# GpSimd waits, at every fourth gather, for the group of four gathers before

## What is computed

```python
# layer 0, graph attention, 8 heads of 64; h = relu(layernorm(x))
feat = h @ W[head]
logit = leaky_relu(alpha_s[src] + alpha_d[dst], 0.2)
att = segment_softmax(logit, by=src)
x = x + relu(segment_sum(att[:, None] * feat[dst], by=src))
# layer 1; h = relu(layernorm(x)), xn = batchnorm(h)
agg = segment_sum(xn[src], by=dst) / max(degree, 1)
conv = relu(agg @ W_conv + b_conv)
attn = linear_attention(h, over 256 rows) @ Wo, taken back by position
x = x + batchnorm(conv + attn + h)
```

## Time and profile before

| | |
|---|---|
| median of 3 runs | 3542.48 us |
| lowest and highest | 3540.49, 3546.79 us |
| the profiled execution, its own time | 3542.78 us |
| its span | 3541.0 us |
| mean granted TensorE clock | 0.883 of full speed |
| busy: TensorE, VectorE, GpSimd, ScalarE | 2699.5, 2161.8, 1858.0, 995.2 us |
| gathers of the first stage (L506), first and last start | 880, 411.5 to 1865.1 us |
| gathers of the second stage (L1133), first and last start | 784, 2070.4 to 3237.6 us |

### The profile page before, as it was taken

The page is one execution under the profiler, slowest core; times in us unless marked ns, Lnnn a source line. Parts: engine busy times, 40 slices in busy tenths (PEclk is TensorE's granted clock), DMA queues, the critical chain, the costliest instruction groups (busy, mean ns, idle before and its releaser), DMA issues. The chain is left out here.

```text
span 3541.0 us, 46052 instructions
## 1 busy us (share of the span) xinstructions
PE 2699.5 (76%) x10647; PEld 1671.1 (47%) x10692; DVE 2161.8 (61%) x3783; ACT 995.2 (28%) x3078; POOL 1858.0 (52%) x1883
## 2 busy tenths in 40 slices
PE   6887377777777877777777787877778788788991
PEld 4554256666656656655656652323333333233440
DVE  9999966666666767666668743333333333334668
ACT  6733334444443444434444520000000000000220
POOL 0000255555555556555555446666666666664667
PEclk8998678898988899898898897888889999999995
DMA  5110366666666666666665856666666666565226
GB/s 184 47 40 31 111 180 185 186 189 185 180 182 188 180 191 189 183 192 176 177 189 191 288 152 174 176 180 178 178 176 178 173 173 175 171 174 157 67 66 251
DMA packets 243449, 588.25 MB, mean 166 GB/s; under 512 B 57744, under 2 KB 82832, under 8 KB 243400
## 3 DMA queue, kind: packets, MB, share of 16 engines
q0 software_dynamic: 133120, 443.52, 43.8%
q1 hardware_dynamic: 110280, 144.14, 12.4%
HBM read 533.43 MB, written 54.10 MB: 166 GB/s over the span
## 5 line engine op out<-in xcount | busy, mean ns | idle before, releaser
L506 POOL DMA_INDIRECT big<-feat_table,idx x880 | 841.3, 956 | 1020.8 <-ACT idx L531 407.5
L1133 POOL DMA_INDIRECT big<-h_table,idx x784 | 743.6, 948 | 460.6 <-issue 235.2
L801 PE MATMUL psA<-big,onehot 128*128 128x260 f32 x1760 | 504.0, 436 | 120.1 <-DVE big L683 95.4
L801 PE MATMUL psB<-big,onehot 128*128 128x260 f32 x1760 | 479.8, 420 | 18.6 <-DVE acc L693 13.1
L801 PEld LDWEIGHTS psA<-big,onehot 128*128 128x128 f32 x1760 | 365.4, 216 | 208.3 <-issue 115.2
L557 ACT ACTIVATE big<-big,late_weights 128x65 f32<-128x65 f32 x1760 | 434.4, 343 | 0.0
L801 PEld LDWEIGHTS psB<-big,onehot 128*128 128x128 f32 x1760 | 351.5, 209 | 84.9 <-DVE acc L693 22.2
L531 ACT CAST idx<-minorB 128x8 int32 (+1 forms) x101 | 20.4, 204 | 1142.6 <-DMA big<-h_table,idx 1142.6
L1565 DVE TENSOR_TENSOR acc<-acc,psCD 128x512 f32 x176 | 120.7, 686 | 320.1 <-remote 106.2
L1565 DVE TENSOR_TENSOR acc<-acc,psA 128x512 f32 x176 | 120.7, 686 | 273.6 <-remote 103.3
L1859 PE MATMUL psA<-big,onehot 128*128 x352 | 199.3, 650 | 58.9 <-issue 42.7
(11 more groups left out here) (447 smaller groups left out, 3960.8 us busy)
## 6 DMA issues: line engine op xcount, KB each, us to landing
nodes_all<-slot_nodes SPq DMA_DIRECT2D x56, 512.0 KB
big<-feat_table,idx POOLq DMA_INDIRECT x880
feat_table<-big SPq DMA_DIRECT2D x49, 264.0 KB, 2.1
x_table<-acc SPq DMA_DIRECT2D x49, 256.0 KB, 3.8
h_table<-big SPq DMA_DIRECT2D x49, 256.0 KB, 4.0
big<-h_table,idx POOLq DMA_INDIRECT x784
big<-h_table SPq DMA_DIRECT2D x49, 256.0 KB, 2.6
big<-x_table SPq DMA_DIRECT2D x49, 256.0 KB, 4.3
```

Of the source, the lines that this page charges most:

```text
L506: g.indirect_dma_start(ring[:, b.k, q * SB + u, :], None, feat_table, bass.IndirectOffsetOnAxis(ap=idx[:, 2 * b.k + q, u:u + 1], axis=0)). ...
L801: ins = pet.matmul(psum[:, 512 * hf:512 * hf + HALF_W], onehot[:, q, u % SB, :], ring[:, b.k, u, HALF_W * hf:HALF_W * (hf + 1)], start=(u ...
L1133: g.indirect_dma_start(big[:, place:place + D], None, h1_table, bass.IndirectOffsetOnAxis(ap=idx[:, r.c % CHUNK_CYCLE, b:b + 1], axis=0)). ...
```

## The change

GpSimd gets one more wait at each fourth gather of a group (gathers 3, 7, 11 and 15 of a batch, 3 and 7 of a row): for the landing of the four gathers of the group before. At that point the three gathers of its own group have been issued after those. Each wait is followed by an increment of `hold`. The first group of each stage has no wait.

```diff
         def layer0_gpsimd(pool):
+            def wait_group_before(b, group):
+                if group > 0:
+                    pool.wait_ge(rows_arrived[b.k * ARRIVAL_GROUPS + group - 1], b.pair(16 * ARRIVAL_GROUP, 16 * ARRIVAL_GROUP))
+                elif b.c > 0:
+                    last = Batch(b.i, b.c - 1)
+                    pool.wait_ge(rows_arrived[last.k * ARRIVAL_GROUPS + ARRIVAL_GROUPS - 1],
+                                 last.pair(16 * ARRIVAL_GROUP, 16 * ARRIVAL_GROUP))
+                elif b.i is not None:
+                    pool.wait_ge(rows_arrived[2 * ARRIVAL_GROUPS - 1], b.pair(16 * ARRIVAL_GROUP, 0))
+                else:
+                    return
+                pool.sem_inc(hold, 1)
...
+                            if (q * SB + u) % ARRIVAL_GROUP == ARRIVAL_GROUP - 1:
+                                wait_group_before(b, (q * SB + u) // ARRIVAL_GROUP)
                             g.indirect_dma_start(ring[:, b.k, q * SB + u, :], None, feat_table,
...
+            def wait_half_before(r, hf):
+                if hf == 1:
+                    group = 2 * r.c % GROUPS1
+                    pool.wait_ge(h_arrived[group], r.turn(64, 64 + arrived_before[group]))
+                elif r.c > 0:
+                    group = (2 * r.c - 1) % GROUPS1
+                    pool.wait_ge(h_arrived[group], Row(r.i, r.c - 1, CHUNK_CYCLE).turn(64, 64 + arrived_before[group]))
+                elif r.i is not None:
+                    pool.wait_ge(h_arrived[GROUPS1 - 1], r.turn(64, arrived_before[GROUPS1 - 1]))
+                else:
+                    return
+                pool.sem_inc(hold, 1)
...
                     for b in range(4 * hf, 4 * hf + 4):
+                        if b == 4 * hf + 3:
+                            wait_half_before(r, hf)
                         place = places[(r.c * SB + b) % RING1]
                         g.indirect_dma_start(big[:, place:place + D], None, h1_table,
```

## The result

The kernel before took 3541.12 us (median of 10 runs, 3529.73 to 3555.16) and the changed one 3556.65 us (10 runs, 3548.09 to 3570.18): a ratio of 1.0048, 95% interval 1.0029 to 1.0068. The change costs 0.5%. The forecast was 3545.0, a gain or loss that could not be told from none, with 3537 to 3554 as its range and 0.82 on "same"; the result is slower by more than its interval, and 2.65 us outside the range.

What follows compares the result with a forecast made beforehand. Second-stage gather issue on GpSimd was taken to be close to the path. Terms 0.6 + 0 + 4 + 0 = 4.6 us on GpSimd, counted at 55%, gave +2.5 us: 3545.0 us, range 3537 to 3554.

Steps and rivals of the forecast that it cites:

- Steps 1 and 2: Second stage: landing 3.70 us plus launch 0.8 us passes before the gather is due at 5.01; two late, 0.6 us.
- rival B: Waits end late: launch of 1.6 us would cost 134 free second-stage groups 0.3 us each, 40 us; chance 0.06.
- rival C: Fewer queued gathers land sooner, 3.43 instead of 3.70 us, 26 us faster in the second stage; chance 0.04.
- Step 3: Added instructions on GpSimd's sequencer: some 0.1 us per group, hidden by running gathers, 0 us; upper end 20 us.
- rival A: GpSimd's sequencer pays at the end of each loop turn in the second stage: 26 us slower; chance 0.08.
- Step 4: Second stage: eight sequencer pauses of 2.4 us show by 0.8 us each with less run-ahead; 4 us on GpSimd.
- Step 5: First stage: waits pass in time, even beside SP's node loads, and 5 us slack per batch absorbs delays; cost 0.
- The share of 55%: Part of GpSimd's 4.6 us delay taken to reach the kernel's time, since waits for freed places shorten: +2.5 us.
- The signs: Second stage: gathers 1.25 us apart, next to no DMA idle, landings 3.7 us, about 8 pauses, at most 1182 us.

Runs made afterwards that it cites:

- e17: The changed kernel again, on a chip where the kernel before takes 3006.45 us: 3080.02 us, ratio 1.0244.
- e3: Kernel before plus the change's waits in both stages, each for the group before the previous one: 3565.99 us, ratio 1.0032.
- e5: Kernel before plus eight increments of `hold` ahead of each fourth gather, both stages, no waits: 3574.65 us, ratio 1.0084.
- e10: Kernel before plus eight increments of `hold` ahead of each third gather, both stages, no waits: 3572.17 us, ratio 1.0083.
- e9: Kernel before plus one increment of `hold` ahead of each fourth gather, both stages, no waits: 3541.88 us, ratio 0.9997.
- e13: Kernel before (3003.62 us on this chip) plus waits for the group three before, ahead of each fourth gather: 3003.95 us, ratio 0.9999.
- e18: The code of e5 on a chip where the kernel before takes 3006.45 us: 3005.37 us, ratio 1.0.
- e4: The changed kernel again, on a chip where the kernel before takes 3548.24 us: 3558.17 us, ratio 1.0024.
- e12: The changed kernel again, on a chip where the kernel before takes 3543.26 us: 3552.2 us, ratio 1.0024.
- e7: Kernel before plus the change's waits in the first stage only, ahead of each third gather: 3542.22 us, ratio 0.9986.
- e11: Kernel before plus the change's waits in both stages, ahead of each third gather: 3531.43 us, ratio 0.997.
- e15: The code of e11 on a chip where the kernel before takes 3003.62 us: 3344.96 us, ratio 1.1135.
- e2: Kernel before plus the change's waits in the second stage only: 3553.07 us, ratio 1.0021.

## Why the prediction was wrong

**Steps 1 and 2, landing and launch in the second stage: right.** 3.76 us against the 3.70 read from before, a launch of 0.77 us, one gather late where two were expected, 0 on the chip without VectorE's stops. So neither rival B (waits that end late) nor rival C (landings sooner; the median is 3.70 us as before) is what happened in this stage; B's mechanism came up in the first stage of e17.

**Step 3, the instructions themselves cost 0: this is the step that failed for the measured time.** It gave each pair of wait and increment 0.1 us on the sequencer, hidden by the gathers, with 20 us as the upper end if the cover were gone. On the chips with the stops they are not free. e3, whose waits hold no gather, costs 0.32% (0.06 to 0.58). e5 and e10 put a plain increment at 8.9 ns on average, which would make 5.0 us for the change; and the change is 10.3 us slower than e9, which has its increments and not its waits. On the other kind of chip the same things cost nothing (e13, e18). The step looked for the cost in GpSimd's own schedule, where it is indeed covered. What carries it into the time where VectorE has its stops isn't shown. The Trainium skill ("Runtime: NRT & Kernel Launch", Instruction fetch mechanics) says that a taken branch to a target outside the two pages at hand stops execution until that page has been fetched. It stood beside the prediction's rival A, a stop at each turn of GpSimd's loop, 26 us; no such stop came in the second stage: the pauses are still one in four turns. Whether VectorE's stops are of this kind no run here tests.

**Step 4, the pauses of the sequencer: right, in kind and nearly in size.** It said that the pauses of 2.4 us, eight in the stage, would show by 0.8 us each once the sequencer can't run ahead. e17 shows eight at 0.7 us, 5.7 us beyond the usual gap at that place. On the chip of the result such gaps are less clean, because four were seen before: at the second gather of a turn there are 4.9 us beyond the usual gap in before and 6.5 in the changed kernel (the one late gather adds 0.65), where 4 were added in the sum; e4 and e12 have 11.0 and 7.7. But e3 has 7.6 and e5 7.2 with their run-ahead intact, so on these chips the pauses can't be put down to the lost run-ahead alone. An example that answers to the earlier trace rows, with the same 1.88 us:

```profile
2209.73 0.95 POOL L1163 DMA_INDIRECT big<-h_table,idx  x1 [1.88 <-issue]
```

**Step 5, the first stage at cost 0: right about the waits on the chip of the result, for a reason that fails elsewhere.** The prediction named the very thing, a landing of more than 5.3 us while SP loads the nodes, and dropped it because "the waits that span such a load have at least 6.08 us of spacing". That spacing was no property of the kernel. It goes with the stops on that chip, where GpSimd waits for slots. Where the gathers run at their own rate the spacing is 5.01 us, the landing is 5.60, and each batch pays. On the chip of the result no wait of the first stage stopped its gather in the profile: the shortest way from a new hold to its gather is 1.06 us there from the third batch on, above the launch. And the slack that the step counted on does exist on such chips: in e7 some 180 third gathers of the first stage start 0.77 us behind the new wait, held by it, and the ratio is 0.9986. That the step's 0 for these waits came true there was luck in the choice of chip.

**The share of 55%: wrong both ways.** On the chips with the stops a delay is repaid by the wait for freed places (e11: 93 us of late gathers, the stage 7 us shorter); on the others it is paid in full (e15: 334 us, 341 paid).

**The size.** The forecast was +2.5 us, the result +15.5; the same kernel gave +9.9 (e4) and +8.9 (e12) on two more chips, about 0.33% over the three if each is weighed by its interval. Of these some 12 us, 5.0 are instructions by e5's price (an estimate, as said). The second stage is 4.3 us longer in the mean of its profiles (1173.2, 1171.7, 1166.0, and 1176.5 of e2, against 1167.2, 1167.1, 1168.7, 1170.1 and 1164.8 where nothing or one increment was added there), and the four differ by 10.5 us among themselves. The rest, in the first stage, stays open: single profiles spread over 25 us there. So the term that was mis-sized is step 3's 0: e3, with nothing held, has a loss as large as the whole (0.32%, some 11 us). How it divides between waits, register operations and increments no run separates further.

**The signs.** All that the prediction set as signs of being right held in the profile, apart from the count of pauses (5 gaps over 1 us at the second gather of a turn, not 8): gathers at 1.25 us, 13.7 us put down to a DMA, landings at 3.7 us, and 1173 us for the second stage, well under 1182. They all watched GpSimd's second stage, and so could not see a loss of which, by the means above, the greater part lies outside it.

**The range.** "The three runs span 6.3 us" was taken for the noise. On one chip thirty runs of the kernel before span 34 us (3528.03 to 3562.25), and its medians differ by 7 us from chip to chip. Three runs that agree say little about a kernel whose executions differ by 1%.

## What to carry to other kernels

Before an idle gap is counted as slack, ask what makes the gap: here the 6.08 us between gathers go with stops of other engines that were seen on some chips only, and where they are missing a wait "with time to spare" holds a gather in each batch. A throttle on landings must be checked against the slowest landing of the loop (5.6 us, under another queue's 512 KB) and against the engine's own rate (5.0 us), not against the spacing in one trace. A wait for a group further back (e13) holds nothing and costs nothing where GpSimd is the bound; one gather earlier (e15) costs 11%, and a gain of 0.3% on other chips (e11) is no reason to take it: neither version here is better than the kernel before on both kinds.

## What was not expected of the hardware

- **Two kinds of chip, one program:** 3541 to 3548 us against 3004 and 3006 us. The one kind has stops of VectorE and ScalarE with no releaser in the trace (VectorE: 306 us of 950 in the second stage's window), the other none. Whether it is the chip or what else went on there at that hour wasn't separated. TensorE's mean granted clock is 0.883 in the one (TensorE 76% busy) and 0.947 in the other (84%, e13).
- **A plain increment on GpSimd costs 8.9 ns on average on the one kind,** in the first stage nearly all of it, and nothing that can be measured on the other (e18).
- **Indirect gathers of the second stage land 3.7 us after their start on both kinds** (median); in the first stage of e17 it is 5.6 us when 512 KB come in on SP's queue beside them.
- **GpSimd's sequencer has its pause at a fixed place,** every 96 gathers of the second stage (gather 97, 193, 289, ...), at the same gathers whatever was added ahead of them. On the chips without the stops it shows only when a wait keeps the sequencer from running ahead (e17: eight gaps; e13 and e18: none).
